# Summing the last layer's messages as columns, and counting targets in message passing

## Time and profile before

| | us |
|---|---|
| runs | 5432.78, 5454.24, 5471.36 |
| median | 5454.24 |
| profiled execution, span from first to last instruction | 5458.0 |
| TensorE / VectorE / ScalarE / GpSimd busy | 4332.6 / 3587.2 / 2141.5 / 2901.1 |
| message passing, first gather to last matmuls | 858.7 to 2292 |
| last layer, first gather to last projection | 2299.6 to 3186 |

### The profile page before, as it was taken

One profiled execution on the slowest core, in us unless ns is written; L12 is line 12 of the kernel. 1 busy time (PEld: TensorE's weight loads), 2 busy tenths in 40 slices (PEclk: granted clock), 3 DMA queues, 4 the chain that ended last, 5 costly groups with the idle time before them and its releaser, 6 DMA issues. The chain is left out here.

```text
span 5458.0 us, 111849 instructions
## 1 busy us (share of the span) xinstructions
PE 4332.6 (79%) x23759; PEld 2886.3 (53%) x23858; DVE 3587.2 (66%) x12001; ACT 2141.5 (39%) x4806; POOL 2901.1 (53%) x2863
## 2 busy tenths in 40 slices
PE   5666664888867888689999967777777775999998
PEld 2444443666645666556666635555555553444444
DVE  7566653444434444478888847667766765899998
ACT  0222221444433444323333323232323332777777
POOL 0555555555535555354444335555555553777775
PEclk9888887999979999989999977777877777999999
DMA  0333334666646666568888744444544443444443
GB/s 18 125 123 131 127 126 119 189 192 186 188 139 184 188 190 189 172 195 266 266 262 264 241 154 134 131 134 130 143 132 129 135 132 92 117 125 128 126 128 99
DMA packets 693097, 852.73 MB, mean 156 GB/s; under 512 B 149445, under 2 KB 511032, under 8 KB 692916
## 3 DMA queue, kind: packets, MB, share of 16 engines
q1 hardware_dynamic: 580020, 631.94, 35.7%
q0 software_dynamic: 112896, 218.94, 16.7%
HBM read 451.91 MB, written 398.61 MB: 156 GB/s over the span
## 5 line engine op out<-in xcount | busy, mean ns | idle before, releaser
L760 POOL DMA_INDIRECT mp_gathered<-msg_rows,other_idx x784 | 752.4, 960 | 659.0 <-PE bank L776 211.1
L776 PE MATMUL bank<-mp_edge_hot,mp_gathered 128*128 128x256 bf16 x3528 | 539.7, 282 | 203.1 <-issue 166.0
L1066 POOL DMA_INDIRECT ll_gathered<-msg_rows,other_idx x392 | 376.1, 959 | 479.1 <-PE bank L1085 228.8
L526 POOL DMA_INDIRECT by_window<-so_pay,so_pos_i x392 | 397.7, 1015 | 435.5 <-issue 299.0
L1372 POOL DMA_INDIRECT at_kv<-kv_rows,kv_idx x392 | 375.6, 958 | 456.3 <-PE bank L1403 176.4
L776 PEld LDWEIGHTS bank<-mp_edge_hot,mp_gathered 128*128 x3528 | 349.8, 99 | 349.2 <-issue 294.3
L879 DVE TENSOR_TENSOR mp_msg_out<-mp_rest,mp_msg_out 128x256 bf16<-128x256 f32 x392 | 166.8, 425 | 490.5 <-ACT mp_msg_out L837 290.7
L824 ACT ACTIVATE mp_h_out<-bank,mp_b_agg 128x256 f32<-128x256 f32 x392 | 185.8, 474 | 714.5 <-PE bank L794 321.6
L1670 POOL DMA_INDIRECT ff_agg<-at_rows,last_idx x392 | 385.8, 984 | 115.9 <-issue 103.0
L1374 POOL DMA_INDIRECT at_q<-q_rows,node_idx x392 | 371.8, 948 | 130.2 <-issue 130.2
L856 DVE TENSOR_SCALAR mp_edge_hot<-digits,mp_first_col,column 128x256 bf16<-128x256 bf16 x1176 | 346.7, 357 | 80.3 <-issue 62.0
(11 more groups left out here) (258 smaller groups left out, 10199.2 us busy)
## 6 DMA issues: line engine op xcount, KB each, us to landing
msg_rows<-mp_msg_out SPq DMA_DIRECT2D x392, 192.0 KB
mp_h_in<-h_cols SPq DMA_DIRECT2D x392, 128.0 KB
h_cols<-mp_h_out SPq DMA_DIRECT2D x392, 128.0 KB
kv_rows<-ll_proj SPq DMA_DIRECT2D x98, 512.0 KB
msg_rows<-so_msg_out SPq DMA_DIRECT2D x98, 384.0 KB
h_cols<-so_h_out SPq DMA_DIRECT2D x98, 256.0 KB
ll_h_in<-h_cols SPq DMA_DIRECT2D x196, 128.0 KB
x_rows<-ll_x_b SPq DMA_DIRECT2D x98, 256.0 KB
```

The costliest lines, as they stand in the source:

```text
L526: pool.indirect_dma_start(core.by_window, bass.IndirectOffsetOnAxis(ap=pos_i[k][:, t:t + 1], axis=0), pay[k][:, t, :], None, bounds_check= ...
L760: pool.indirect_dma_start(gathered[:, r * PARTS * D:(r + 1) * PARTS * D], None, core.msg_rows[layer % 2], bass.IndirectOffsetOnAxis(ap=cor ...
L776: product = nc.tensor.matmul(agg_bank[k], gathered[:, bass.ds(at + d * D, D)], hot, start=(first and d == 0), stop=True, skip_group_check= ...
L1066: pool.indirect_dma_start(gathered[:, r * PARTS * D:(r + 1) * PARTS * D], None, core.msg_rows[(LAYERS - 1) % 2], bass.IndirectOffsetOnAxis ...
```

## The change

The last layer sums as message passing does: gathered rows stationary, one-hots moving, 9 matmuls of 256 columns, one own product. ScalarE closes each group with relu and bias into `sums` (new step `close_group`), TensorE transposes the four tiles of it into one bank (`turn_sums`), and VectorE adds x to that. ScalarE evicts three projection tiles of four. The offsets of the later steps grow by two blocks, SyncE's store by one group. Targets are counted in message passing, one tile of 128 edges per block and layer instead of two per block in the last layer. The bias of W_agg is loaded once, one value per partition; its three-part split and the bias matmul go. The diff, cut:

```diff
...
+                pe.wait_ge(zero_ok, 1)
+                nc.tensor.matmul(count_bank, zero_cols[:, 0:NG], zero_cols[:, :], start=True, stop=True)
...
+                    def count_targets(n, r, j):
+                        pe.wait_ge(dst_hot_ok, wins + n + 1)
+                        for odd in range(2):
+                            counted = nc.tensor.matmul(count_bank[:, odd * W:(odd + 1) * W], hi_hot[r % RING][:, odd::2], lo_hot[r % RING][:, :],
+                                                       start=False, stop=True, skip_group_check=True)
+                        counted.then_inc(dst_mm, 1)
+
                     def turn(do):
                         do(0, sum_edges)
+                        do(0, count_targets)
                         do(-1, edge_product)
                         do(-2, messages)
...
+                nc.vector.memset(zero_cols[:, :], 0.0).then_inc(zero_ok, 1)
...
+                    def target_hots(n, r, j):
+                        reached(dve, dst_mm, wins + n - RING + 1)
+                        nc.vector.tensor_scalar(lo_hot[r % RING][:, :], core.digits[:, :], core.dst_lo[:, bass.ds(wins + n, 1)], None, ALU.is_equal)
+                        nc.vector.tensor_scalar(hi_hot[r % RING][:, :], core.digits[:, 0:NW], core.dst_hi[:, bass.ds(wins + n, 1)], None,
+                                                ALU.is_equal).then_inc(dst_hot_ok, 1)
+
                     def turn(do):
                         do(0, hots)
                         do(-5, low_part)
                         do(-4, rest_part)
+                        do(0, target_hots)
                     blocks(dve, turn, MSGS)
+                dve.wait_ge(dst_mm, 2 * NW)
+                nc.vector.tensor_copy(core.dst_count[0:NG, :], count_bank).then_inc(tabs_ok, 1)
...
-    NPJ, HOTS, TURN, BY_ACT = 3 * D, 8, 8, 2
+    NPJ, HOTS, TURN, BY_ACT = 3 * D, 8, 8, 3
     Q = TURN // 2
-    rows_bank, x1_bank, proj_bank = bank[2:4], bank[0], [bank[1], bank[4], bank[5], bank[7]]
-    count_bank = bank[6][0:NG, :]
+    sums_bank, rows_bank, x1_bank, proj_bank = bank[2:4], bank[6], bank[0], [bank[1], bank[4], bank[5], bank[7]]
...
-            for n in range(NW + 10):
+            for n in range(NW + 14):
                 if n + RING - 1 < NW:
                     reached(sp, block_mm, n)
                     load_h(n + RING - 1)
                 if n % 2 == 0 and n // 2 + Q - 1 < NG:
                     reached(sp, y_ok, n // 2)
                     load_x(n // 2 + Q - 1)
-                if n % 2 and 0 <= n // 2 - 4 < NG:
-                    store(n // 2 - 4)
+                if n % 2 and 0 <= n // 2 - 5 < NG:
+                    store(n // 2 - 5)
...
+            def block_sums(r):
+                return sums_bank[r // 2 % 2][:, r % 2 * W:(r % 2 + 1) * W]
+
+            def add_tile(r, i, hot, first=False):
                 at = (i & (TILES - 1)) * (PARTS * D)
-                for half in range(2):
-                    to = rows_bank[r // 2 % 2][:, (r % 2 * 2 + half) * P:(r % 2 * 2 + half + 1) * P]
-                    for d in range(PARTS):
-                        product = nc.tensor.matmul(to, hot(half), gathered[:, bass.ds(at + d * D, D)], start=False, stop=True, skip_group_check=True)
+                for d in range(PARTS):
+                    product = nc.tensor.matmul(block_sums(r), gathered[:, bass.ds(at + d * D, D)], hot, start=(first and d == 0),
+                                               stop=True, skip_group_check=True)
                 return product
 
             def sum_edges(n, r, j):
...
                 if r % 2 == 0:
-                    reached(pe, y_ok, Q * j + r // 2 - 1)
-                    nc.tensor.matmul(rows_bank[r // 2 % 2][:, :], core.ones[0:PARTS, :], agg_parts[:, :], start=True, stop=True, skip_group_check=True)
+                    reached(pe, sums_ok, Q * j + r // 2 - 1)
                 pe.wait_ge(edge_hot_ok, n + 1)
                 pe.wait_ge(tile_in, first + ALWAYS)
                 for c in range(ALWAYS):
-                    added = add_tile(r, first + c, lambda half: edge_hot[r % HOTS][:, c, half * P:(half + 1) * P])
+                    added = add_tile(r, first + c, edge_hot[r % HOTS][:, c, :], first=c == 0)
                 added.then_inc(tile_mm, 1)
                 further(pe, n, first, final, more)
                 pe.wait_ge(h_ld[r % RING], 16 * (TURN // RING * j + r // RING + 1))
-                for half in range(2):
-                    own = nc.tensor.matmul(rows_bank[r // 2 % 2][:, (r % 2 * 2 + half) * P:(r % 2 * 2 + half + 1) * P],
-                                           h_in[r % RING][:, half * P:(half + 1) * P], w_agg_h[:, :], start=False, stop=True, skip_group_check=True)
-                own.then_inc(block_mm, 1)
...
+                nc.tensor.matmul(block_sums(r), w_agg_h[:, :], h_in[r % RING][:, :], start=False, stop=True,
+                                 skip_group_check=True).then_inc(block_mm, 1)
+
+            def turn_sums(g, q, j):
+                pe.wait_ge(sums_ok, g + 1)
+                reached(pe, y_ok, g)
+                for t in range(T):
+                    last = nc.tensor.transpose(rows_bank[:, t * P:(t + 1) * P], sums[q % 2][:, t * P:(t + 1) * P], ident[:, :])
+                last.then_inc(sums_t, 1)
 
...
             def turn(do):
                 do(0, sum_edges)
-                do(0, count_targets)
-                do(-6, group(turn_x1))
-                do(-8, group(project))
+                do(-2, group(turn_sums))
+                do(-8, group(turn_x1))
+                do(-10, group(project))
             blocks(pe, turn)
 
...
+            def close_group(g, q, j):
+                act.wait_ge(block_mm, 2 * g + 2)
+                reached(act, sums_t, g - 1)
+                nc.scalar.activation(sums[q % 2][:, :], sums_bank[q % 2][:, :], ACT.Relu, bias=agg_bias[:, 0:1]).then_inc(sums_ok, 1)
 
             def roots(g, q, j):
                 act.wait_ge(mom_ok, g + 1)
...
             def turn(do):
-                do(0, group(roots))
-                do(-4, group(x1_columns))
-                do(-2, group(normalize))
-                do(-6, group(evict))
+                do(0, group(close_group))
+                do(-4, group(roots))
+                do(-8, group(x1_columns))
+                do(-6, group(normalize))
+                do(-10, group(evict))
...
             def add_rows(g, q, j):
-                dve.wait_ge(block_mm, 2 * g + 2)
+                dve.wait_ge(sums_t, g + 1)
...
-                nc.vector.scalar_tensor_tensor(out=y[q][:, :, :], in0=rows_bank[q % 2][:, :].rearrange("p (t f) -> p t f", t=T), scalar=0.0,
-                                               in1=x_in[q][:, :, :], op0=ALU.max, op1=ALU.add).then_inc(y_ok, 1)
+                nc.vector.tensor_tensor(y[q][:, :, :], rows_bank[:, :].rearrange("p (t f) -> p t f", t=T), x_in[q][:, :, :], ALU.add).then_inc(y_ok, 1)
...
             def turn(do):
-                do(-3, group(add_rows))
-                do(-6, group(deviations))
-                do(-8, group(add_b2))
-                do(-10, group(add_biases))
+                do(-5, group(add_rows))
+                do(-8, group(deviations))
+                do(-10, group(add_b2))
+                do(-12, group(add_biases))
                 do(0, hots)
-                do(0, target_hots)
             blocks(dve, turn)
-            dve.wait_ge(dst_mm, NW)
```

More of the change, by code:

```diff
@@ L651, in message_passing @@
         msg_out = sb("mp_msg_out", [P, MSGS, 2, PARTS, D], BF16)
-        wts, tabs_ok = core.sem("mp_weights_in"), core.sem("mp_place_tables")
+        lo_hot, hi_hot = ([sb(f"mp_{n}_hot{r}", [P, width], BF16) for r in range(RING)] for n, width in (("lo", W), ("hi", NW)))
+        zero_cols = sb("mp_zero_cols", [P, GR], BF16)
+        wts, tabs_ok, zero_ok = core.sem("mp_weights_in"), core.sem("mp_place_tables"), core.sem("mp_zeros_ready")
+        dst_hot_ok, dst_mm = core.sem("mp_dst_hots"), core.sem("mp_dst_counted")
         h_ld, h_st = ([core.sem(f"mp_{n}{r}") for r in range(RING)] for n in ("h_loaded", "h_stored"))
@@ L1004, in _ @@
             sp.dma_start(w_agg_h[:, :], W_agg[D:2 * D, :]).then_inc(wts, 16)
-            for t in range(T):
-                sp.dma_start(agg_bias[:, t, :], b_agg.partition_broadcast(PARTS)).then_inc(wts, 16)
+            with nc.allow_non_contiguous_dma(reason="one bias value per partition"):
+                sp.dma_start(agg_bias[:, :], b_agg.rearrange("(p a) -> p a", a=1)).then_inc(wts, 16)
             for n, name in enumerate(("Wk", "Wv", "Wq")):
@@ L1074, in _ @@
         def _(pe):
[L1075 to L1080 removed]
+            pe.wait_ge(wts, 9 * 16)
+            pe.wait_ge(parts_c, 7)
+            def block_sums(r):
+                return sums_bank[r // 2 % 2][:, r % 2 * W:(r % 2 + 1) * W]
+            def add_tile(r, i, hot, first=False):
                 at = (i & (TILES - 1)) * (PARTS * D)
[L1082 to L1085 removed]
+                for d in range(PARTS):
```

(23 more changed lines are left out.)

31 lines of the change are left out of this document (11 added, 20 removed).

## The result

The changed kernel takes 5475.35 us (median of 6 runs, 5460.23 to 5482.35) against 5453.74 (6 runs) before: ratio 1.0047 [1.0028, 1.0067], about 26 us slower by the ratio (the medians differ by 21.6).

| us | before | after | forecast |
|---|---|---|---|
| message passing, first to last own product (L794; L800 after) | 1421.2 | 1443.6 | +47 |
| last layer, first gather to attention's first gather | 901.6 | 909.5 | -58 |
| last layer, mean period of groups 13 to 97 | 8.52 | 8.59 | -0.70 a group |

What follows compares the result with a forecast made beforehand. TensorE was taken to bound both stages, by its matmul list in the last layer and its instruction queue in message passing. -61 + 3 + 47 = -11, with the half-clock start about -16 us: 5438 us; range 5380 to 5510.

Steps and rivals of the forecast that it cites:

- So this stage is worth what TensorE's list of matmuls costs: Last layer: TensorE has no idle time, so shorter matmul work shortens a group from 8.25 to 7.55 us.
- 98 groups pay it: Last layer: every group pays TensorE's matmul list; about 87 of 98, in the dense stretch, save 0.70 us each, -61 us.
- Both stay below 7.5: Last layer: after the change VectorE (about 5.5 us a group) and ScalarE (about 1.1 on 3.3) stay below 7.5 us.
- Message passing, +47: Message passing: the added count costs TensorE 0.12 us a block over 392 blocks, +47 us.
- the one-hots' wait: Message passing: TensorE's added wait for VectorE's target one-hots before counting, costed at nothing.
- +3 us for the deeper pipeline: Last layer: one group of projections moves to the tail, between 0 and +4 us, taken as +3.
- few us less for the half-clock start: Start of the last layer, at half clock: a few us less, taking the sum from -11 to about -16 us.
- A: Rival, chance 0.24: message passing's idle array hides the count at cost 0; the last layer's gain stands alone, 5396 us.
- B: Rival, chance 0.14: last layer bound by a ring of loads, store landing and VectorE steps, 7.0 to 8.4 us; up to 5504.
- C: Rival, chance 0.08: in message passing TensorE pays for the whole count, 0.32 us a block, +125 us; 5521 us.
- D: Rival, chance 0.03: in message passing VectorE's moved one-hots lock GpSimd out and slow gathers, at most +78 us, 5516.
- E: Rival, chance 0.09: the change misses its aim, for instance TensorE's last-layer time not shrinking; half the gain goes, 5470 us.

## Why the prediction was wrong

The forecast was 5438, faster by 16 us; it became slower by about 26. The sign was wrong; the size stayed within 1% and inside the range.

*"So this stage is worth what TensorE's list of matmuls costs"* is the step that failed, and with it "98 groups pay it". The total of the list came out: 0.67 us a group measured without gathers, 0.70 forecast, though by luck, since the count was worth 0.55 instead of 0.88 and the rest 0.12 instead of -0.18. But the stage took 8 us more, not 58 less. The prediction saw in message passing that TensorE's register instructions reach 727 ns and put it down to TensorE's own queue in that stage. It comes with the gathers, which the last layer has as well. While the last layer's gathers came in pairs and its list was long, the delay cost nothing (8.52 us with gathers, 8.54 without). With the count gone it costs 0.24 us a group (8.23 against 7.99), and with the column sum, whose gathers come in fours as in message passing, 0.72 us, the whole gain.

Two thirds of that, 0.48 us, reached TensorE by VectorE's order, which the prediction never asked about. Of VectorE and ScalarE it said "Both stay below 7.5", which was true of VectorE (417 of 640 us busy) and beside the point, since its one-hots waited, they were not slow. That the longer list before hid the delay is argued from these periods; the shorter delay of a pair is measured, and the share of each is not known.

*Message passing, +47*: +22.4 us in the profiled pair, 0.06 us a block instead of 0.12. On two other chips, by traces of kernels that differ in the last layer alone otherwise, it is 7 and 10 us (mean of three 1414.7 against 1407.9; 1409.5 against 1399.3). Since traces of the same code differ by up to 10 us, these two do not tell the count's cost from nothing; the doubled count, 35.5 us, does show that added matmuls cost something. The mechanism was right, the array idles and takes most of it; the value belonged nearer to the low end. No run shows a cost of the one-hots' wait.

*+3 us for the deeper pipeline*: the stage grew by 7.9 us and its 84 periods by 5.5 (715.7 to 721.2), which leaves 2.4 for front and tail. For the "few us less for the half-clock start" the prediction shows no row, and it did not come: the granted clock stayed below 1.00 from 2300 to 2360 us before and from 2320 to 2400 after.

*The signs.* Both stages moved in the same direction, which the prediction had named as a sign that it is wrong.

*The rivals.* A's first half came near, a count that costs little; its gain in the last layer did not come. B, the store ring: both of its signs came, VectorE's wait for the store (57.6 us) and a group of over 8 us, and it was still not B: taking that wait away changed nothing, since the wait for the projection took its place. C: not the 0.32 us. D, GpSimd locked out by VectorE: gathers take 971 and 962 ns against 962 and 958 in the earlier trace rows, 1% at most, so nothing here shows the rule that was weighed. E was the right one, with a chance of 0.09 and 5470 us: "TensorE's order of time not shrinking in the last layer because the shorter blocks are then held by its queue as in message passing". It lacked the cause and the price: the whole gain went, not half. The stalls' sum of 59.4 us is close to the gain forecast, but it is no price: with VectorE's order changed there are more of them (76.1 us) and the period is 0.48 us shorter.

## What to carry to other kernels

Where TensorE is 98% busy beside gathers, matmuls taken out of its list need not shorten the stage: look for register instructions far above their median on its queue in a stage with the same gathers, look whether the gathers come in longer bursts there, and measure the gain with and without them. In the turn of an in-order engine, try to put what the bottleneck waits for ahead of a step that waits for the bottleneck: one moved line was worth 0.48 us of 8.59. It has to be measured: moved further, to the head of the turn, the same line kept only 0.16. And of a change with two halves, time each: here the count's move alone won 0.35%, and the column sum lost it.

## What the runs showed of the hardware

- While GpSimd issues indirect gathers (962 ns each), TensorE's register instructions, 46 ns in the median, can take about 0.7 us: 85 times in 600 us of after, where the gathers come in bursts of four; once before, where they come in pairs; never in three kernels without gathers, never with plain loads of as many bytes.
- TensorE's semaphores rise late beside such gathers, mostly 0.8 to 1.5 us after the end of a burst: 0.74 us late in the median before, 3.02 after, 0.01 without gathers or with plain loads. The Trainium skill, "Perfetto Trace Analysis", section "Summary: the profiler window per engine type", lists a semaphore's way as hidden from TensorE's rows; the trace agrees, the delay shows only in the waiters' idle time (1.82 us of VectorE) and in the semaphore records.
- The second sum of 18 matmuls of a group, 1.01 us in before, took 1.32 us once the count was gone, with gathers and without (the count moved alone).
